# Routing of a switch layer on one core: transposes of consecutive batches in two bank sets, and logits directly behind their encoder products

## The reference

```
x_enc = layernorm(h) @ enc_w + enc_b              # 192 -> 64
logits = x_enc @ sw_w + sw_b                      # 64 -> 8 experts
routes = argmax(softmax(logits)); p = max(softmax(logits))
hid = gelu(einsum('td,edr->ter', layernorm(h), w1) + b1)   # 8 x 64
out = (hid * onehot(routes)) @ w2 + onehot(routes) @ b2
h = h + out * p
```

## Time and profile before

| | us |
|---|---|
| runs: 1373.02, 1375.83, 1375.84; median | 1375.83 |
| the profiled execution, its own time | 1372.88 |
| its span in the profile | 1371.1 |
| the block of the switch layer, in the span | 261.2 to 366.7 |
| its routing part, from the first fill to the end of the last logits | 261.35 to 296.29 |

### The profile page before, as it was taken

One profiled execution on the slowest core, in us unless ns is written; L12 is line 12 of the kernel. 1 busy time (PEld: TensorE's weight loads), 2 busy tenths in 40 slices (PEclk: granted clock), 3 DMA queues, 4 the chain that ended last, 5 costly groups with the idle time before them and its releaser, 6 DMA issues. The chain is left out here.

```text
span 1371.1 us, 29272 instructions
## 1 busy us (share of the span) xinstructions
PE 1252.3 (91%) x11347; PEld 862.8 (63%) x11347; DVE 912.3 (67%) x2294; ACT 729.3 (53%) x1529; POOL 381.5 (28%) x445
## 2 busy tenths in 40 slices
PE   4889999799779999899999998899986899899998
PEld 3532333345647777677777776777864445588888
DVE  6588888413578777799888877888874899400001
ACT  1446555432224443688888884788874334443310
POOL 6500000100057777456666660000000344200000
PEclk9889999979989999999999999999998999999999
DMA  3342121300024234634343452122102300177811
GB/s 99 106 124 70 47 61 34 72 15 1 21 74 124 82 117 128 204 111 124 109 132 98 140 137 64 41 64 59 47 1 93 129 1 1 39 274 276 281 69 46
DMA packets 99287, 127.42 MB, mean 93 GB/s; under 512 B 24590, under 2 KB 87805, under 8 KB 94957
## 3 DMA queue, kind: packets, MB, share of 16 engines
q1 hardware_dynamic: 96556, 123.44, 29.5%
q0 software_dynamic: 1536, 1.59, 0.5%
q10 hardware_dynamic: 1056, 0.52, 0.1%
HBM read 89.06 MB, written 37.88 MB: 93 GB/s over the span
## 5 line engine op out<-in xcount | busy, mean ns | idle before, releaser
L1792 POOL TENSOR_SCALAR r_grD<-gr 32x192 f32<-32x192 f32 x192 | 101.8, 530 | 93.8 <-DVE gr L1686 45.9
L700 ACT ACTIVATE PT<-bank 128x1024 f32<-128x1024 f32 x96 | 94.3, 1023 | 59.5 <-PE bank L580 58.8
L641 DVE TENSOR_REDUCE mx<-bank 128x1 f32<-128x512 f32 x176 | 110.0, 682 | 12.2 <-PE bank L563 11.9
L1523 PE MATMUL bank<-r_grD,ek 128*128 128x256 f32 x384 | 100.0, 396 | 0.0
L2554 DVE TENSOR_TENSOR eo_all<-bank,m_b2s 128x768 f32<-128x768 f32 x8 | 7.7, 958 | 138.5 <-PE bank L2515 138.5
L2546 ACT ACTIVATE x_g<-bank,m_b1s 128x128 f32<-128x128 f32 x192 | 51.4, 399 | 75.7 <-PE bank L2497 75.7
L1523 PEld LDWEIGHTS bank<-r_grD,ek 128*128 128x128 f32 x384 | 67.7, 189 | 9.3
L2428 POOL TENSOR_SCALAR m_xs<-m_xs 128x256 f32<-128x256 f32 x4 | 2.5, 632 | 247.6 <-DVE m_xs L2319 247.6
L1736 ACT ACTIVATE r_t<-r_xh,r_cd 128x64 f32<-128x64 f32 x192 | 70.2, 429 | 0.8
L1514 PEld LDWEIGHTS bank<-gr,r_A 128*128 128x128 f32 x384 | 47.6, 190 | 33.7 <-DVE gr L1686 32.6
L1352 POOL TENSOR_TENSOR rope_c<-cy,p_rope 128x512 f32<-128x512 f32 x48 | 60.0, 1270 | 20.0 <-DVE cy L1205 20.0
(11 more groups left out here) (380 smaller groups left out, 3235.3 us busy)
## 6 DMA issues: line engine op xcount, KB each, us to landing
wb<-in_m_w SPq DMA_DIRECT2D x32, 1152.0 KB, 5.6
ek<-k_d SPq DMA_DIRECT2D x32, 384.0 KB
k_d<-t_late SPq DMA_DIRECT2D x46, 256.0 KB, 2.8
tgt<-c_d SPq DMA_DIRECT2D x33, 196.0 KB
c_d<-t_late SPq DMA_DIRECT2D x32, 196.0 KB, 2.9
g_d<-gr SPq DMA_DIRECT2D x32, 192.0 KB
o_G<-g_d SPq DMA_DIRECT2D x32, 192.0 KB, 3.0
qk_d<-a_parts SPq DMA_DIRECT2D x24, 192.0 KB, 3.0
```

The costliest lines, as they stand in the source:

```text
L641: v.tensor_reduce(mx[u % 2][:, j // 4, j % 4:j % 4 + 1], slot(f"A{u}.{j}"), AX.X, ALU.max).then_inc(*dve.did(f"max{u}.{j}"))
L700: a.activation(PT[kt % 2][:, 2 * hp:2 * hp + 2, :], STB[s % 2][:, :, :], ACT.Exp, scale=DH ** -0.5)\
L1523: last = t_.matmul(SP_[g][:, i * B * E1:(i + 1) * B * E1], ek[r][:, p, :], grD[g][:, i, :, :].rearrange("p b e -> p (b e)"), start=False, ...
L1792: last = g_.tensor_scalar(grD[g][rr, :, b, :], b3(gr[j % RING][rr, cols(g)]), 0.0, None, ALU.bypass)
```

## The change

TensorE's loop becomes: encoder products of b, `turn(b + 1)`, logits of b. `turn` uses the banks `ps[0:2]` for even and `ps[4:6]` for odd batches, and waits for the copy of the batch before the last instead of the last one. Seven fills ahead of `turn(0)` become four, and one more follows it. ScalarE does the root of batch 1 ahead of the copy of batch 0. The lists of names follow.

```diff
--- before.py
+++ after.py
@@ -770,6 +770,7 @@
         cols = lambda b: slice(b * N, (b + 1) * N)
         lg_ps = ps[3][:, 0:TILES * E0].rearrange("p (t e) -> p t e", t=TILES)
         bc = lambda ap, n: ap.unsqueeze(2).to_broadcast([P, ap.shape[1], n])
+        TBANK = [ps[0:2], ps[4:6]]
         HBANK, MBANK, HOTBANK = ps[4:6], ps[6:8], [ps[2], ps[0], ps[1], ps[2]]
         YLAG = 2
         STATS = {0: (1, 2), 1: (3,), 2: (), 3: ()}
@@ -782,12 +783,11 @@
                        ([f"hid{k}"] if k < len(K) else ["nrs", "nxn"] if k == len(K) else [])
                        + ([f"{n}{(k - YLAG) // CE}" for n in (("res", "nst", "nag") if (k - YLAG) // CE < B - 1 else ("res",))]
                           if k >= YLAG and (k - YLAG) % CE == CE - 1 else [])])
-        act = Steps(sem("f_act_s"), ["std0", "xT0", "std1", "std2", "xe0", "xT1", "std3", "xe1", "xT2", "xe2", "xT3", "xe3",
+        act = Steps(sem("f_act_s"), ["std0", "std1", "xT0", "std2", "xe0", "xT1", "std3", "xe1", "xT2", "xe2", "xT3", "xe3",
                                      "ex"] + [f"hotT{b}" for b in SB] + [f"gelu{k}" for k in K] + ["nroot"])
         lined = sem("f_lined")
-        pe = Steps(sem("f_pe"), ["T0"] + [n for b in SB for n in ([f"T{b + 1}"] if b + 1 < B else [])
-                                          + [f"enc{b}"] + ([f"lg{b - 1}"] if b else [])]
-                   + ["lg3", "h0", "h1"] + [f"hotT{b}" for b in SB]
+        pe = Steps(sem("f_pe"), ["T0"] + [n for b in SB for n in [f"enc{b}"] + ([f"T{b + 1}"] if b + 1 < B else []) + [f"lg{b}"]]
+                   + ["h0", "h1"] + [f"hotT{b}" for b in SB]
                    + [n for k in range(len(K) + YLAG) for n in
                       ([f"mask{k}"] if k < len(K) else []) + ([f"h{k + 2}"] if k + 2 < len(K) else [])
                       + ([f"y{(k - YLAG) // CE}"] if k >= YLAG and (k - YLAG) % CE == CE - 1 else [])])
@@ -816,11 +816,11 @@
 
                 def turn(b):
                     t_.wait_ge(*dve.at(f"xn{b}"))
-                    if b:
-                        t_.wait_ge(*act.at(f"xT{b - 1}"))
+                    if b >= 2:
+                        t_.wait_ge(*act.at(f"xT{b - 2}"))
                     for c in range(KC):
                         for t in range(TB):
-                            last = t_.transpose(ps[c][0:DC, t * P:(t + 1) * P], xn[:, b * TB + t, c * DC:(c + 1) * DC], ident[:, :])
+                            last = t_.transpose(TBANK[b % 2][c][0:DC, t * P:(t + 1) * P], xn[:, b * TB + t, c * DC:(c + 1) * DC], ident[:, :])
                     last.then_inc(*pe.did(f"T{b}"))
 
                 def logits(b):
@@ -857,22 +857,21 @@
                         last = t_.matmul(y, hotT[:, b, t * P:(t + 1) * P], b2p[:, :], start=False, stop=True)
                     last.then_inc(*pe.did(f"y{b}"))
 
-                fill(t_, ps[7], ident, 7)
+                fill(t_, ps[7], ident, 4)
                 turn(0)
+                fill(t_, ps[7], ident, 1)
                 t_.wait_ge(enc_in, 80)
                 t_.wait_ge(lined, 1)
                 for b in SB:
-                    if b + 1 < B:
-                        turn(b + 1)
                     t_.wait_ge(*act.at(f"xT{b}"))
                     if b:
                         t_.wait_ge(*act.at(f"xe{b - 1}"))
                     for kc in range(KC):
                         last = t_.matmul(ps[2][0:R0, :], enc_w[:, kc, :], xT[:, kc, cols(b)], start=(kc == 0), stop=(kc == 1))
                     last.then_inc(*pe.did(f"enc{b}"))
-                    if b:
-                        logits(b - 1)
-                logits(B - 1)
+                    if b + 1 < B:
+                        turn(b + 1)
+                    logits(b)
                 t_.wait_ge(rest_in, 112)
                 hidden(0)
                 hidden(1)
@@ -998,7 +997,7 @@
                 def out_of(b):
                     a.wait_ge(*pe.at(f"T{b}"))
                     for c in range(KC):
-                        last = a.activation(xT[:, c, cols(b)], ps[c][0:DC, :], ACT.Copy)
+                        last = a.activation(xT[:, c, cols(b)], TBANK[b % 2][c][0:DC, :], ACT.Copy)
                     last.then_inc(*act.did(f"xT{b}"))
 
                 def encoded(b):
@@ -1006,8 +1005,8 @@
                     a.activation(xe[0:R0, cols(b)], ps[2][0:R0, :], ACT.Identity, bias=enc_b[:, 0:1]).then_inc(*act.did(f"xe{b}"))
 
                 root(0)
+                root(1)
                 out_of(0)
-                root(1)
                 root(2)
                 a.wait_ge(enc_in, 80)
                 encoded(0)
```

## The result

The changed kernel took 1359.51 us (median of four runs, 1358.84 to 1363.46), beside 1374.42 us (1371.59 to 1375.84) for the kernel before: a ratio of 0.9881, with a 95% interval of 0.9854 to 0.9908. In a second group of runs it took 1360.73 beside 1380.14 us, a ratio of 0.9864 (0.9838 to 0.9891). The ratios are taken over the single runs and are not the quotients of the two medians, which are 0.9892 and 0.9859. The direction was forecast. By the medians the gain is 15 and 19 us; I had taken 11 for the routing, and 12.3 from the median then known (1375.83 to 1363.5).

What follows compares the result with a forecast made beforehand. Bound: TensorE's chain up to the last logits, for which VectorE idles 16.00 us. Logits 11.4 plus hidden products 2.2 give 13.6 us; with the clock falling at the end, 11 taken: 1363.5 us, range 1359.3 to 1370.0.

Steps and rivals of the forecast that it cites:

- Head of the stage: Routing start: four fills let batch 0's transposes (T0) run 1.6 us earlier; its encoder products (enc0) start at 268.7, not 272.51.
- the rival of the late loads: Small loads delay the first encoder product to 271.3; everything 2.6 us later, gain 8 us, 1365 to 1368; chance 0.06.
- Order: TensorE's routing loop: copies lie under other work, so a batch costs 4.1 us at the full clock, not 5.0.
- the second bank pair is worth 0: Transposes in the routing loop: encoder products already waited for the copy, so another bank pair gains and costs nothing.
- the swap costs 0.6 without a return: ScalarE, routing start: root of batch 1 ahead of batch 0's copy delays the copy 0.6 us; VectorE is busy anyway.
- Hidden 0 and 1: Hidden products behind the last logits: 5.78 us mostly at low clock, 3.6 at full clock, so 2.2 us more gain.
- S gain 10.7 forecast: S runs from first fill to one-hot transposes; gain 10.7 us if last logits and hidden products run at the low clock.
- The clock: Routing on TensorE: closer packing with encoder work between keeps the granted clock at 1.00 to about 281, low near the end.
- rival A: Routing clock falls early, TensorE becomes the bound at 7.2 us a batch; gain between 0 and 5.9 us; chance 0.17.
- the slower case (B): Clock falls between fills and first encoder product, staying low through the one-hot transposes and fills: 1377 to 1380; chance 0.05.
- the row that I took for logits and transposes ahead of the fall at 283.6: Old routing stretch 280.2 to 283.6, busy 2.56 of 3.40 us before the clock fell; read as showing kind of work counts.
- some 6 of the 11.4 are clock: Last logits end 11.4 us earlier; the old order at full clock would end near 290, so some 6 us are clock.

Runs made afterwards that it cites:

- the old order at the full clock: The kernel before with identity products in all of TensorE's waits, three more behind the transposes of batch 0: 1370.62 us, ratio 0.9916.

## Why the prediction was right in its mechanism and wrong in its size

*Head of the stage.* Right. T0 was forecast 4.45 us behind the first fill and came at 4.42; enc0 7.35, measured 7.27. The small loads were there: enc0 followed the copy, so the rival of the late loads did not happen.

*Order.* Right: 4.1 us a batch forecast and 4.08 to 4.11 measured, the last logits' end at 23.55 forecast and at 23.33. That the second bank pair is worth 0 and that the swap costs 0.6 without a return held (0.00 and 0.43).

*Hidden 0 and 1.* In the first profile they ran at the low clock, as I took it (S gain 10.7 forecast, 10.49 measured); in others at the full one (13.6 forecast from 40.58, 13.9 measured). That 10.7 came so close is partly luck: it took 0.7 us off for last logits at the low clock, which ran at the full one (1.06 us), and nothing for hidden products slower than before, which took 7.07 us where the old kernel's took 5.95.

*The clock.* The direction held: from the first transposes to the last logits (to 0.1 us) it was at 1.00 in every profile of the new order. So the early fall (rival A) did not occur in any of them, nor the slower case (B). On the trace, transposes and logits with encoder work between them kept the level for 18.9 us (from T0 to the last logits), and transposes ran at both levels, 1.04 and 1.92 us for eight. The Trainium skill (TensorE: Matmul & The Clock Gate, Part 4) says that the full level doesn't engage for transposes and that they don't count as busy in the same way. By the reading that I gave it, as rival A, the gain would have been 0 to 5.9 us; that is not what these runs show, as far as the whole mixture goes. No run here had transposes alone. And the row that I took for logits and transposes ahead of the fall at 283.6 also held the end of the encoder products of batch 1 (277.71 + 3.17 = 280.88), so it spoke less for the kind of work than I said.

*The step that failed* is the term "some 6 of the 11.4 are clock", and with it the sum against one profiled execution. For the profile that it was read from the term was right: to the end of the last logits the first profile of before took 34.94 us and the old order at the full clock 29.17, so 5.8 us are clock, and 5.8 of the order (5.4 forecast). But I read the low stretches of the old kernel, 3.4 and 17.1 us, as a property of the kernel. They are one draw: three profiles had 20.5, 27.3 and 34.1 us of low clock within the routing, and the one I had was the mildest. In the other two the last logits end 36.89 and 39.36 us after the first fill, so the term measured 7.7 and 10.2 us there. With hidden 0 and 1 the clock was worth 8.0, 10.3 and 12.4 us of S in the three, where the sum of 11 rests on the first alone. With the 5.9 of the order the stretch gives 14 to 18 us where the clock stays up to the end, and up to 3.4 less where hidden 0 and 1 fall back. A lesser term was left out: the last output products, 1.3 us in the first pair of profiles. The lower end of the range, 1359.3, took in what the changed kernel's clock might do, but left the old kernel's clock as it was drawn; that the first median still fell inside it, by 0.2 us, is luck.

Open stays how much of the last few us between the stage (mean 107.1 us in three profiles of before, 93.6 in both of the changed kernel, so 13.5) and the medians (15 to 19) is the same draw in executions without a profile, how much is the chip (the kernel before had medians of 1374.42 to 1380.43 us over the groups), and how much is chance: the intervals of the ratio reach from 12.7 to 22.3 us at 1376 us.

## What to carry to other kernels

Where the granted clock falls inside a stretch full of small waits, its low time in one profile is a sample: profile the kernel before several times before a gain is sized. The mean clock of an execution is a weaker sign, since it is taken over the whole kernel: it was 0.965 in the second profile of before and 0.963 in the first, though S was 2.3 us longer in the second. Order TensorE's queue so that the product whose operand is ready comes first and the copy of its result lies under the next piece of work; that shortens the chain, and here it closed the holes ahead of the falls. A second buffer is worth something only if, in the new order, its wait would still be the last to end.

## What the runs showed of the hardware that I had not expected

The same instructions in the same order took 40.6, 42.9 or 45.0 us for the routing, by the clock alone; with the waits filled with identity products they took 32.55. In the second profile of before a short stretch at 1.00 lay between two at 0.50.

```profile
263.20:274.50 11.30, 8.21 (x31) 4.42 (x32) 9.47 (x48) 2.94 (x6) 3.37 (x4) 1.00 0.72 181
274.50:291.60 17.10, 15.20 (x35) 6.71 (x36) 5.14 (x20) 3.47 (x7) 0.00 (x0) 0.50 0.20 53
291.60:295.00 3.40, 2.66 (x13) 1.43 (x12) 0.00 (x0) 1.64 (x3) 0.00 (x0) 1.00 0.02 5
295.00:305.20 10.20, 10.20 (x25) 5.61 (x24) 2.30 (x9) 2.27 (x3) 0.00 (x0) 0.50 0.00 0
```

At the low level TensorE was busy for 31.64 of 34.10 us in the third profile, in its last 24.3 us for 24.28, and the clock did not come back within them, while the changed kernel held 1.00 with 17.23 of 20.00. In part the larger share is an effect of the level: the same encoder products take 3.68 us at the low one and 1.93 at the full one. And the embedding stage at the start (from its first product to the first of the next block), whose code no kernel here touches, took between 78.5 and 89.4 us from profile to profile, with 3 to 24 us of low clock that do not account for it (89.4 us came with 13.7 at the low level, 79.4 with 3.4, 78.5 with 14.4). What does was not tried. Behind the switch layer the profiles differ by 3 us at most (1002.8 to 1005.9), so among the profiled executions of the new order, 1355.50 to 1372.90 us, this first stage is most of the spread.
